# Attention and gated feed-forward layer: projection blocks moved into the score banks, and a reordered branch

## The reference

```python
# x: (2, 1024, 512); 32 query heads, 8 key/value heads, head size 16
Q, K, V = x@Wq.T+bq, x@Wk.T+bk, x@Wv.T+bv        # split in heads
Q, K = rope(Q, K)
w = softmax(Q K^T / 4)                            # per head, 1024 x 1024
attn = (w V) heads joined
x = layernorm(x + attn @ Wo.T + bo)
h = silu((x @ gate_w.T)*gate_s) * ((x @ up_w.T)*up_s)   # inner size 1408
out = layernorm(x + (h @ down_w.T)*down_s)
```

## Time and profile before

| what | us |
|---|---|
| runs (3) | 1166.45, 1172.8, 1174.82; median 1172.8 |
| the profiled execution, its time | 1173.22 |
| its span, first to last instruction | 1171.3 |
| TensorE busy | 1090.3 (93%) |
| VectorE busy | 788.0 (67%) |
| ScalarE busy | 636.9 (54%) |
| GpSimd busy | 203.0 (17%) |
| mean granted TensorE clock | 0.970 |

### The profile page before, as it was taken

How to read it: one execution, slowest core, us unless ns; L and a number is a source line. 1 busy time by engine, 2 the same in 40 slices (tenths; PEclk the granted TensorE clock), 3 DMA queues, 4 the chain that set the end, 5 groups by cost and what they waited for, 6 DMA issues and landing times. The chain is left out here.

```text
span 1171.3 us, 14733 instructions
## 1 busy us (share of the span) xinstructions
PE 1090.3 (93%) x5660; PEld 541.6 (46%) x5660; DVE 788.0 (67%) x884; ACT 636.9 (54%) x1191; POOL 203.0 (17%) x165
## 2 busy tenths in 40 slices
PE   8999999999899999998999999999789899999995
PEld 3533333333333533333333333333236478878884
DVE  5769869996769768675668999999303345362534
ACT  2148767886667567662467878778453022222221
POOL 1150062101230020400012005960000100000002
PEclk9979999999799999999999999999799999999998
DMA  5065416326133231511015246610205020000000
GB/s 217 38 150 141 97 48 143 77 68 141 47 69 92 45 69 64 102 54 32 10 49 105 61 138 135 184 43 28 94 10 164 0 90 37 1 1 36 1 36 36
DMA packets 36588, 86.44 MB, mean 74 GB/s; under 512 B 12512, under 2 KB 12896, under 8 KB 34432
## 3 DMA queue, kind: packets, MB, share of 16 engines
q1 hardware_dynamic: 35936, 84.71, 27.9%
q10 hardware_dynamic: 576, 0.72, 0.2%
HBM read 48.71 MB, written 23.86 MB: 62 GB/s over the span
## 5 line engine op out<-in xcount | busy, mean ns | idle before, releaser
L424 DVE TENSOR_REDUCE nmx<-PSA 128x1 f32<-128x1024 f32 x512 | 600.3, 1217 | 121.8 <-PE PSA L413 121.4
L492 ACT ACTIVATE Bn<-PS 128x512 f32<-128x512 f32 x1024 | 530.1, 605 | 204.0 <-PE PS L486 203.7
L486 PE MATMUL PS<-Qt,Kt 50*128 50x512 f32 x1024 | 384.3, 457 | 40.1 <-ACT Bn L492 22.8
L413 PE MATMUL PSA<-Kt,Qt 48*128 48x512 f32 x1024 | 397.9, 470 | 8.7 <-DVE nmx L424 7.5
L486 PEld LDWEIGHTS PS<-Qt,Kt 50*128 50x128 f32 x1024 | 172.7, 189 | 346.3 <-ACT Bn L492 297.7
L505 PE MATMUL PV<-Bn 128*32 128x512 f32 x2048 | 281.9, 623 | 0.0
L413 PEld LDWEIGHTS PSA<-Kt,Qt 48*128 48x128 f32 x1024 | 168.7, 188 | 45.8 <-DVE nmx L424 27.8
L995 PE MATMUL PSA<-x1Th,wr 128*128 128x512 f32 x344 | 136.5, 397 | 0.5 <-DVE sg L1015 0.5
L995 PE MATMUL PSA<-x1Tl,wr 128*128 128x512 f32 x344 | 135.2, 393 | 0.0
L1015 DVE SCALAR_TENSOR_TENSOR sg<-PSA,us,sg 128x512 f32<-128x512 f32 x43 | 32.1, 749 | 137.7 <-ACT sg L1006 137.5
L1006 ACT ACTIVATE sg<-PSA,gs 128x512 f32<-128x512 f32 x43 | 29.5, 689 | 165.1 <-PE PSA L995 165.1
(11 more groups left out here) (121 smaller groups left out, 603.6 us busy)
## 6 DMA issues: line engine op xcount, KB each, us to landing
Qt<-pscr SPq DMA_DIRECT2D x90, 128.0 KB, 5.5
A<-in_wf SPq DMA_DIRECT2D x11, 768.0 KB, 6.9
wr<-A SPq DMA_DIRECT2D x33, 256.0 KB, 2.7
pscr<-A SPq DMA_DIRECT2D x16, 512.0 KB, 3.9
vscr<-Bn SPq DMA_DIRECT2D x32, 256.0 KB, 2.0
Kt<-pscr SPq DMA_DIRECT2D x90, 64.0 KB, 2.4
A<-in_xT SPq DMA_DIRECT2D x4, 1024.0 KB, 8.8
A<-A SPq DMA_DIRECT2D x16, 256.0 KB, 3.7
```

The lines of the kernel that those rows point to most:

```text
L413: r = pe.do(lambda e, h=h, p=p: e.matmul(ps[:, h, :], Qt[i][p:p + NC_, g % 2, 128 * qt:128 * qt + 128], Kt[i][p:p + NC_, 512 * h:512 * h + ...
L424: r_mxs[hh, s] = dve.do(lambda e: e.tensor_reduce(nmx[:, hh % 2, c0:c0 + 1], ps, AX.XY, ALU.max, negate=True), c_rel[s])
L486: r = pe.do(lambda e: e.matmul(PS2[:, c % 3, :], Kt[i][rows, 128 * kt:128 * kt + 128], Qt[i][rows, g % 2, 512 * qh:512 * qh + 512], start= ...
L492: r_exp[c] = act.do(lambda e: e.activation(Pb[c % NP_], PS2[:, c % 3, :], ACT.Exp, scale=0.25), c_exp)
```

## The change

What it does, part by part:
1. `Queue.run`: the condition is turned round, `exact` is the `If` part and `full` the `Else` part.
2. `free2` holds, for the three score banks and `PV`, what must be over before each is written. `project` and `values` no longer take a `PSA` slot: they write bank `s2n % 3` (the next score's) with the first half and bank `(s2n + 2) % 3` (the last score's) with the second, and each half is taken out as soon as it is complete (ScalarE for `project`, two operations of 512 columns; VectorE for `values`). `scores` waits for `free2` of its bank alone, `weigh(0)` for `PV`.
3. `out_project(0, t2)` does the same, with a VectorE addition for each half. In `out_project(1, t2)` the slot stays, and the addition is by halves too.
4. In `unit` the background blocks run after `weigh(u-1)` and no longer before it.
5. The norms of an `out_project(0, t2)` are issued as a whole in the next block's unit, after its scores and before its `weigh`.
6. Blocks stand at w = 3 or w = 11: projections at (1,11), (4,3), (5,3), (6,3), (8,3), (11,3), `values(1)` at (6,11), output projections at (9,3), (9,11), (10,3), (10,11), norms at (9,11), (10,3), (10,11), (11,3). The load of batch 1's `xT` goes from (4,0) to (3,0). The gaps of 6 and 2 units stay.
7. At the start `project(0, 1)` writes banks 2 and `PV`, `project(0, 2)` bank 0 and `PV`, each half taken out at once; the second query half is evacuated before the first is placed.

```diff
-        with e.If(low_bits > 0):
-            for f in self.full:
+        with e.If(low_bits < 1):
+            for f in self.exact:
                 f(e)
         with e.Else():
-            for f in self.exact:
+            for f in self.full:
                 f(e)
...
+        free2 = [(), (), (), ()]
+        s2n = [0]
+        def bank2(i):
+            return PS2[:, i, :] if i < 3 else PV[:, :]
+        def next_banks():
+            return s2n[0] % 3, (s2n[0] + 2) % 3
...
+        def project(b, m, banks=None):
+            fine = banks is not None
+            banks = banks or next_banks()
             i = qn[0] % 2
             qn[0] += 1
             raw, qrot = qraw[i], qrots[i]
...
+            for h in range(2):
+                ps = bank2(banks[h])
+                pe.wait(*free2[banks[h]])
+                for k in range(KT):
+                    r = product(ps, b, m, h, k, c_fill if k == KT - 1 else None)
+                    if fine and (h, k) != (1, KT - 1):
+                        if k == KT - 1:
+                            evacuate_raw(m, raw, h, ps, r, i, banks)
+                        yield
+                r_ev = evacuate_raw(m, raw, h, ps, r, i, banks) if h == 1 or not fine else None
             sp.wait(r_ev)
...
+        def evacuate_raw(m, raw, h, ps, r, i, banks):
+            act.wait(r, r_bqk, *free_raw[i])
+            r = act.do(lambda e: e.activation(raw[:, 512 * h:512 * h + 512], ps, ACT.Identity, bias=bqk[:, m:m + 1]), c_ev)
+            free2[banks[h]] = (r,)
+            return r
...
-            pe.wait(r_exp[c - 3] if c >= 3 else r_idle[-1])
+            pe.wait(*free2[c % 3])
...
+            free2[c % 3] = (r_exp[c],)
...
         def out_project(b, t2):
-            s, ps = slot()
             pe.wait(r_late["wo"])
+            if b == 0:
+                banks = next_banks()
+                halves = [bank2(i) for i in banks]
+            else:
+                s, ps = slot()
+                halves = [ps[:, j, :] for j in range(2)]
+            rows = [x1[b][:, 2 * t2 + j, :] for j in range(2)]
             for j in range(2):
                 t = 2 * t2 + j
+                if b == 0:
+                    pe.wait(*free2[banks[j]])
...
+                dve.wait(r, r_xb[b])
+                y = dve.do(lambda e, j=j: e.tensor_tensor(rows[j], rows[j], halves[j], ALU.add),
+                           c_y if b == 0 or j == 0 else c_rel[s])
+                if b == 0:
+                    free2[banks[j]] = (y,)
...
+            if b == 0:
+                yield
+            yield from normalise(rows, rows, [y], c_x1, lambda r: r_x1.__setitem__((b, t2), r))
...
-        spread(project(0, 3), 1, 10, (6, 2))
+        spread(project(0, 3), 1, 11, (6, 2))
...
-        put(4, 0, load_b1)
-        spread(project(1, 4), 4, 8, (6, 2))
-        spread(project(1, 0), 5, 4, (6, 2))
-        spread(values(1), 6, 14, ())
+        put(3, 0, load_b1)
+        spread(project(1, 4), 4, 3, (6, 2))
+        spread(project(1, 0), 5, 3, (6, 2))
+        spread(values(1), 6, 11, ())
         for m in (1, 2, 3):
-            spread(project(1, m), 2 * m + 5 - m // 2, 2, (6, 2))
+            spread(project(1, m), (0, 6, 8, 11)[m], 3, (6, 2))
...
+        outs = [out_project(0, t2) for t2 in range(4)]
         for t2 in range(4):
-            spread(out_project(0, t2), 9, 3 + 2 * t2, (1,))
+            spread(outs[t2], 9 + t2 // 2, 3 + 8 * (t2 % 2), ())
+        for t2, (n, w) in enumerate(((9, 11), (10, 3), (10, 11), (11, 3))):
+            before[n, w] = lambda t2=t2: whole(outs[t2])
...
                 cur[0] = u
-                for gen in blocks.get((n, w), []):
-                    next(gen)
+                if (n, w) in before:
+                    before[n, w]()
             if u >= 1:
...
                 weigh(u - 1)
             if u < U:
+                for gen in blocks.get((n, w), []):
+                    next(gen)
                 if w == 3:
                     reciprocals()
```

More of the change, by code:

```diff
@@ L346, in place, with values @@
             return q.do(lambda e: e.tensor_copy(dst, src), c_pick[1])
-        def values(b, idle=False, after=()):
-            s, ps = (None, PS2[:, 0:2, :]) if idle else slot()
-            pe.wait(*after)
+        def values(b, banks=None):
+            fine = banks is not None
+            banks = banks or next_banks()
             pe.wait(r_wv)
             for t in range(8):
-                pe.wait(r_xT[b][t // 4])
+                h = t // 4
+                pe.wait(r_xT[b][h], *free2[banks[h]])
                 for k in range(KT):
-                    last = t == 7 and k == KT - 1
-                    r = pe.do(lambda e, t=t, k=k: e.matmul(
-                        ps[:, t // 4, 128 * (t % 4):128 * (t % 4) + 128],
+                    r = pe.do(lambda e, t=t, k=k, ps=bank2(banks[h]): e.matmul(
+                        ps[:, 128 * (t % 4):128 * (t % 4) + 128],
                         xT[:, t // 4, k, 128 * (t % 4):128 * (t % 4) + 128], wv[:, k, :],
-                        start=(k == 0), stop=(k == KT - 1)), c_fill if last else None)
-                if idle and t < 7:
+                        start=(k == 0), stop=(k == KT - 1)), c_fill if t % 4 == 3 and k == KT - 1 else None)
+                if t % 4 == 3:
+                    dve.wait(r, r_bv, r_cst)
+                    v = dve.do(lambda e, h=h, ps=bank2(banks[h]): e.tensor_tensor(
+                        Vp[:, b, 4 * h:4 * h + 4, :, 0:HD],
+                        ps.rearrange("p (t v c) -> p t v c", t=4, v=NKV),
+                        bv[:, :].rearrange("p (o v c) -> p o v c", o=1, v=NKV).to_broadcast([128, 4, NKV, HD]),
+                        ALU.add), c_v)
+                    free2[banks[h]] = (v,)
+                if fine and t < 7:
                     yield
             last_xT[b] = r
[L363 to L369, removed]
             r_vp[b] = v
@@ L605, in out_project @@
                     r = pe.do(lambda e, j=j, k=k, t=t, kc=kc: e.matmul(
-                        ps[:, j, :], AT[kc % 6][:, 128 * t:128 * t + 128], wo[:, k, :],
-                        start=(k == 0), stop=(k == KT - 1)), c_fill if (j, k) == (1, KT - 1) else None)
-            r_pj[b] = r
[L609 to L613, removed]
+                        halves[j], AT[kc % 6][:, 128 * t:128 * t + 128], wo[:, k, :],
+                        start=(k == 0), stop=(k == KT - 1)), c_fill if k == KT - 1 else None)
+                dve.wait(r, r_xb[b])
[3 more added lines that the diff above has]
+                    free2[banks[j]] = (y,)
+            r_pj[b] = r
+            if b == 0:
+                yield
+            yield from normalise(rows, rows, [y], c_x1, lambda r: r_x1.__setitem__((b, t2), r))
         def whole(*gens):
@@ L627, in spread @@
                 background.setdefault(divmod(u, 16), []).append(lambda: next(gen, None))
-        blocks = {}
+        blocks, before = {}, {}
         cur = [0]
@@ L756, in post_ln_layer @@
             else:
[L757 to L758 removed]
+                next(second)
+                next(second)
         gather(1)
[L760 to L761 removed]
+        third = project(0, 2, (0, 3))
         fine = [second, second, *[third] * 8]
```

45 lines of the change are left out of this document (12 added, 33 removed).

## The result

| | before | after |
|---|---|---|
| median, us | 1170.5 (4 runs, 1166.45 to 1174.82) | 1135.41 (4 runs, 1128.81 to 1139.99) |
| profiled execution, us | 1173.22 | 1139.99 |
| its span, us | 1171.3 | 1138.1 |

The ratio is 0.9695, with a 95% interval of 0.9633 to 0.9758: faster by 35 us, where 35.2 were forecast. The two profiled executions differ by 33.2 us of span, which can be laid out over the kernel, because each unit has one group of eight `weigh` products, now on L513 (L505 before). From here on a group is named by the unit whose products it holds. The distance between the same two groups in both traces gives each part's share. It is the share in this one pair of executions; where the clock falls differs from one execution to the next.

The account below looks back on a forecast made before the run. TensorE bounds the kernel, ending last by 0.2 us a unit among three nearly balanced engines. 5.7 + 10.3 + 8.5 + 1.6 + 6.3 + 3.3 - 0.5 = 35.2 us off 1173.22 gives 1138.0, range 1127 to 1152.

Parts of the forecast that it names:

- Part 1: Projection and values blocks: each costs 7.3 us for 7.54; with casts and turns 5.7 us gained, bounds 0 and 8.
- Casts and turns: Beside projection blocks: ScalarE casts avoid the PV copy, 2.6 us gained; turns with reciprocals hide behind blocks, 1.4 us.
- Part 2: Four output projections in the loop: 7.4 us each, 29.6 for an excess of 39.9, so 10.3 us gained.
- half evacuation: Behind a block: the next unit's third score waits on ScalarE's 0.68 us read of the second half; 0.2 us shows.
- Part 3: Turn beside GpSimd's rotation after the (4,8) block: moved apart, 8.5 us gained, bounds 0 and 8.5.
- Rival C: A turn still meets GpSimd through a late transfer; the 8.5 us are not gained, 1146.5 us; chance 0.09.
- Part 4: The start: 1.6 us from the evacuation wait and 6.3 us from full clock without that stop.
- Rival A: The clock still falls at the start because the first two units are thin; 1144.3 us, chance 0.22.
- Part 5: The branch: idle 5.32 us shrinks, 3.3 us gained; the clock's fall is left in; 0.5 us lost at the end.
- rival B: The clock stays up at the branch too, 5.9 us less, 1132.1 us; chance 0.15.
- The end: Kernel's end: SP's jump over `full` stands behind everything, between 0 and 4.8 us, taken as 0.5 us lost.
- Rival E: Score banks become the bound and the clock falls 5.6 us after each of eleven blocks; 1199.6 us, chance 0.04.

Follow-up runs that it names:

- e3: Kernel before with only the new block places and the earlier xT load; 1153.41 us for 1167.09, ratio 0.9866.
- e5: Changed kernel with norms issued right behind their block, one unit to the scaling; 1145.22 us against 1168.6 for the kernel before, ratio 0.9816.
- e12: Kernel before with one block, project(1,4), moved from (4,8) to (4,3) and its load to (3,0); 1159.92 us for 1172.64, ratio 0.9931.
- e7: Changed kernel with project(0, 2)'s rotation waiting for the first turn and low-bit sums in threes behind turns; 1127.68 us against 1168.6 before, ratio 0.9678.
- e1: Kernel before with only the branch turned round; 1160.58 us for 1167.09, ratio 0.9931.
- e4: Changed kernel with the loop's blocks writing PSA slots again; 1135.26 us against 1167.09 for the kernel before, ratio 0.9725.
- e6: Changed kernel with low-bit sums in groups of three tiles, each behind a turn; 1134.02 us against 1172.64 for the kernel before, ratio 0.9679.
- e8: Changed kernel with blocks ahead of weigh again, still in score banks; 1135.14 us against 1168.6 for the kernel before, ratio 0.9719.
- e11: Changed kernel with PSA slots and blocks ahead of weigh both restored; 1137.87 us against 1168.6 for the kernel before, ratio 0.9757.
- e9: Changed kernel with project(0, 1)'s high-part cast on ScalarE two units later; 1140.94 us against 1172.64 for the kernel before, ratio 0.9708.
- e10: Changed kernel with low-bit sums between turns and project(0, 1)'s cast two units later; 1136.41 us against 1172.64 for the kernel before, ratio 0.9692.
- e2: Changed kernel with the old branch order; 1145.07 us against 1167.09 for the kernel before, ratio 0.9801.

## Why the prediction was right, point by point

- **The bound.** TensorE ending last by 0.2 us a unit held: all gains came from places where it stood, and a unit without one takes 2.60 or 2.61 in both.
- **Part 1.** 7.3 a block was forecast, 7.21 measured (9.82 - 2.61). The gain is 0.32 and not 0.24 a block, for the reason given, TensorE's slot wait; but banks and order are two cures of one wait, which the text took as one. Casts and turns gave 2.3 and 1.5, for 2.6 and 1.4.
- **Part 2.** The step was the size of one term: 7.4 a block, where 7.08 was measured, nearly the 7.13 of the block itself. The half evacuation that I let show is hidden. What carried it is now separated: eight units between blocks (e3) and norms inside a block (7.1 us, e5).
- **Part 3.** 8.5 forecast, 8.6 measured, and e12 shows that the one place does it and not the load. Rival C fell for this turn.
- **Part 4** is the step that failed. "Without the stop I expect full clock" named the 1.36 us wait as the fall's only cause. The stop went and gave 2.5 (first group at 70.03), but the next one was GpSimd's, two units later. In the profiled pair 2.6 of the following 5.6 came; over all executions of the old and the new start none of it shows. Rival A was right that the clock still falls, but its reason (thin units) doesn't suffice: e7 has the same thin first units, a stop of 1.87 and no fall. The part put its eye on TensorE's wait and not on what ScalarE and VectorE waited for.
- **Part 5.** The flag's idle time became 1.34 for 1.5 to 2 forecast. The fall was left in at its full 5.9; in the profiled execution it lasted two units and cost less, hence 6.0 for 3.3. In five of the nine experiments with the turned branch it did not come at all (e1, e4, e6, e8, e11: rival B), in the other four one to two units were slow. The end cost nothing, not 0.5. The Trainium skill (Runtime: NRT & Kernel Launch, section "Instruction fetch mechanics") says that a taken branch to a page outside the two held has to fetch it first. "Issue" at 4.71 for the taken and 0.81 for the other branch agrees for the jump ahead of the work. No run here shows a price for one behind it.
- **Not forecast.** Groups 12 to 14 lost 4.6, of which 3.6 are a clock fall that the six other kernels with the same sums did not have there. That 2 us of stalls stand in this stretch, before the change and after it, I had not seen: I followed the rotation of moved blocks to the turns, but not GpSimd's other work. It is rival C at another place; e6 and e7 show cause and cure of the stalls.
- **Rival E.** Blocks cost 9.82 with 2.60 behind. No dip stands behind any of the eleven.

## What to carry to other kernels

Before counting a gain from a removed stop, list what each of the other engines waits for within the next few units, because the next stop in line may be of another kind and bring the same clock fall. Where two engines can hold each other up, tie the free one's work to the other's by a wait (behind the turn) and not by a place in its list: what waits only for its data drifts whenever anything else moves. Before a gain is read from one profiled execution, look at the same stretch in every other run that leaves it as it is: here that takes 3.6 us off one reading and 2.6 off another. Put the side work of the second-busiest engine inside the blocks of the busiest, the only place where it has room.

## What the runs showed of the hardware that was not expected

- A pause of about 1.3 us brings the clock down in some executions and not in others. At the branch 1.27 left it up in e1, e4, e6, e8 and e11, and a unit or two behind 1.26 to 1.28 were slow in e5, e7, e9 and e10; at the start of e7 1.87 did nothing. Where it fell in the attention loop it cost one to four units up to about 1.5 us each.
- Executions of one kernel spread by about 1% with their mean granted clock: 1128.81 at 0.995, 1134.71 at 0.988, 1139.99 at 0.983 for the kernel after. The Trainium skill (TensorE: Matmul & The Clock Gate, section "The HAM clock gate") says that what the chip watches runs freely and doesn't begin with the kernel, so that the same kernel meets it at another point each time. The spread agrees with that; no run here shows it to be the reason.
- Two stalls beside GpSimd can follow each other directly where it is busy without a gap: cast 1.85, then subtraction 2.27 (e9), 4.1 us for two operations of 0.17.
- The branch not taken costs 0.7 to 0.8 us of "issue" on TensorE (0.81 after, 0.72 or 0.73 in nine experiments), the taken one 4.7 to 5.0 (4.78 before and in e3, 4.71 in e2, 5.01 in e12).
